# Cross-attention and linear attention on one core: one visit of values and ones per unit, and one running sum of the exponentials

## The reference, cut to what matters

```python
def layer0(q, k, v):                       # q = x, k = v = ctx
    Q, K, V = (heads(a @ W.T + b) for ...) # 4 x 16 x 1024 x 32
    score = einsum('bhqd,bhkd->bhqk', Q, K) / sqrt(32)
    att = softmax(score, axis=-1)
    out = einsum('bhqk,bhkd->bhqd', att, V) @ Wo.T + bo
    return layernorm(out + q) * gamma0 + beta0

def layer1(query, key, value):             # query = layer 0's result, key = value = ctx
    Q_phi, K_phi = elu(query), elu(key)
    KV = einsum('bnd,bne->bde', K_phi, value)
    Z = 1.0 / (einsum('bnd,bd->bn', Q_phi, K_phi.sum(axis=1)) + 1e-6)
    return layernorm(query + einsum('bnd,bde->bne', Q_phi, KV) * Z[..., None]) * gamma1 + beta1
```

## Time and profile before

| | |
|---|---|
| median of 3 runs | 1592.95 us |
| the profiled execution | 1593.17 us, span 1591.9 us |
| TensorE (PE) busy | 1542.1 us, 97% |
| VectorE (DVE) busy | 1225.6 us, 77% |
| GpSimd (POOL) busy | 1098.2 us, 69% |
| ScalarE (ACT) busy | 821.5 us, 52% |
| value matmuls L469 / ones matmuls L476, busy | 256.2 / 80.5 us |
| mean granted TensorE clock | 0.985 |

### The profile page before, as it was taken

One profiled execution on the slowest core, in us unless ns is written; L12 is line 12 of the kernel. 1 busy time (PEld: TensorE's weight loads), 2 busy tenths in 40 slices (PEclk: granted clock), 3 DMA queues, 4 the chain that ended last, 5 costly groups with the idle time before them and its releaser, 6 DMA issues.

```text
span 1591.9 us, 30289 instructions
## 1 busy us (share of the span) xinstructions
PE 1542.1 (97%) x10912; PEld 1037.1 (65%) x10912; DVE 1225.6 (77%) x2399; ACT 821.5 (52%) x1577; POOL 1098.2 (69%) x1012
## 2 busy tenths in 40 slices
PE   7989999999999999999999999999999999999996
PEld 5756667676766767667676676667667666766552
DVE  3767776767788787976778788886777877798887
ACT  1454554544555555655455455655455555565541
POOL 0365765657778787866678787776678878786881
PEclk9999999999999999999999999999999999999999
DMA  8634235351523426244242524425242342410000
GB/s 241 204 127 141 87 91 162 111 144 42 156 77 104 122 80 187 69 124 130 78 117 64 160 83 125 148 72 155 70 133 74 102 132 89 135 61 28 14 29 33
DMA packets 160340, 171.06 MB, mean 107 GB/s; under 512 B 21824, under 2 KB 122176, under 8 KB 160192
## 3 DMA queue, kind: packets, MB, share of 16 engines
q1 hardware_dynamic: 155968, 167.30, 34.9%
q10 hardware_dynamic: 4224, 1.84, 0.5%
HBM read 126.10 MB, written 42.99 MB: 106 GB/s over the span
## 4 chain that ended last, share of the span: by engine, by line
PE 89%; DVE 4%; DMA 2%; issue 2%; POOL 1%; ACT 1%; SPq 0%; ACTq 0%; DVEq 0%; POOLq 0%
PE score L437 15%; PE acc L469 15%; PE scoreT L451 14%; PE misc L510 7%; PE misc L522 7%; PE misc L486 7%; PE misc L538 7%; PE misc L499 7%; PE misc L546 6%; PE acc L476 3%; DVE maxes L739 1%; PE misc L530 1%; DMA bv_col<-bv_in 1%; ACT p_ring L612 1%; DMA ctx_nat<-ctx_in 0%
## 5 line engine op out<-in xcount | busy, mean ns | idle before, releaser
L969 POOL TENSOR_TENSOR pair_sum<-p_ring 128x512 f32<-128x512 f32 x512 | 664.4, 1308 | 366.4 <-DVE pair_sum L772 209.6
L612 ACT ACTIVATE p_ring<-scoreT 128x512 f32<-128x512 f32 x1024 | 602.1, 596 | 609.1 <-PE scoreT L451 603.8
L739 DVE TENSOR_REDUCE maxes<-score 128x1 f32<-128x512 f32 x1024 | 682.6, 679 | 236.8 <-PE score L437 232.2
L437 PE MATMUL score<-k_stack,q_stack 96*128 96x512 f32 x1024 | 647.0, 632 | 21.8 <-DVE maxes L739 15.6
L451 PEld LDWEIGHTS scoreT<-q_stack,k_stack 104*128 104x128 f32 x2048 | 386.5, 192 | 186.4 <-ACT p_ring L612 106.6
L451 PE MATMUL scoreT<-q_stack,k_stack 104*128 104x256 f32 x2048 | 427.1, 290 | 6.1 <-ACT p_ring L612 5.5
L437 PEld LDWEIGHTS score<-k_stack,q_stack 96*128 96x128 f32 x1024 | 194.1, 190 | 197.3 <-issue 141.6
L469 PE MATMUL acc<-p_ring,v_sb 128*32 128x256 f32 x4096 | 256.2, 392 | 0.0
L469 PEld LDWEIGHTS acc<-p_ring,v_sb 128*32 128x32 f32 x4096 | 122.3, 112 | 89.0 <-issue 9.4
L976 POOL TENSOR_TENSOR pair_sum<-pair_sum 128x512 f32<-128x512 f32 x128 | 163.9, 1281 | 0.0
L510 PE MATMUL misc<-wv,ctxT_sb 128*128 128x128 f32 x1024 | 134.8, 275 | 0.2 <-DVE k_low L812 0.2
(11 more groups left out here) (81 smaller groups left out, 1232.2 us busy)
## 6 DMA issues: line engine op xcount, KB each, us to landing
xT_sb<-xT_in SPq DMA_DIRECT2D x62, 512.0 KB, 3.7
k_stack<-k_dram SPq DMA_DIRECT2D x96, 256.0 KB, 4.2
q_stack<-q_dram SPq DMA_DIRECT2D x192, 128.0 KB, 2.5
k_dram<-k_high SPq DMA_DIRECT2D x32, 256.0 KB, 2.2
k_dram<-k_low SPq DMA_DIRECT2D x32, 256.0 KB, 2.2
q_dram<-q_high SPq DMA_DIRECT2D x64, 128.0 KB, 1.7
q_dram<-q_low SPq DMA_DIRECT2D x64, 128.0 KB, 1.9
ctx_nat<-ctx_in SPq DMA_DIRECT2D x32, 256.0 KB, 4.9
```

What stands on the lines that cost most here:

```text
L437: pe.matmul(score[k % 3][:], q_stack[0:SPLIT, unit % NQ, j, t * P:(t + 1) * P], k_stack[0:SPLIT, group_of[unit] % 2 * QUAD + j, h * HALF:( ...
L612: act.activation(p_ring[:, n % NP, h * HALF:(h + 1) * HALF], scoreT[k % 2][:], ACT.Exp, scale=SCALE).then_inc(A["exped"], 1)
L739: dve.reduce_max(maxes[:, unit % 2, t, j, h:h + 1], score[k % 3][:], AX.X).then_inc(V["maxed"], 1)
L969: pool.tensor_tensor(pair_sum[:, place_of_pair(pair), cols], p_ring[:, (n - 1) % NP, cols], p_ring[:, n % NP, cols], ALU.add).then_inc(L[" ...
```

## The change

One visit per unit in place of two, at `LEAD + 16`, after all eight steps: thirty-two value matmuls, then four ones matmuls over one sum of all eight steps, `exp_sum`. That sum is run up in place, step by step: GpSimd adds the low half of each of steps 1 to 7 and the high half of steps 4, 5 and 6; VectorE adds the high half of steps 1, 2, 3 and 7. `p_ring` grows from 8 places to 9, and an exponential into a place waits for the unit's ones. In the tick of a visit and the one after it the planner books up to 50 units of cost, and in the tick after it the finishing steps stand ahead of that tick's exponential and maximum. Keys' and queries' low halves are kept a tick later, with the DMAs that store them. The choice between the two ends of a layer norm is open to all tiles. Some distances of the planner change with it.

```diff
-    NQ, NP, NO, NX = 3, 8, 19, 3
+    NQ, NP, NO, NX = 3, 9, 19, 3
-    VISIT_AT = LEAD + 13
+    VISIT_AT = LEAD + UT
+    HIGH_ON_POOL = (4, 5, 6)
+    HIGH_ON_DVE = (1, 2, 3, 7)
-        TILE_TICKS = 21
+        TILE_TICKS = 20
...
+        def span(k):
+            return 50 if visiting(k) is not None else 14
         def find(name, engine, k, cost):
-            steps = when.setdefault(name, {})
-            while k in steps or room[engine].get(k, 0) + cost > (26 if visiting(k) is not None else 14):
+            steps, load = when.setdefault(name, {}), room[engine]
+            while k in steps or load.get(k, 0) + cost > span(k) and (
+                    load.get(k, 0) > span(k) - 4 or
+                    load.get(k, 0) + cost + load.get(k + 1, 0) > span(k) + span(k + 1)):
                 k += 1
...
-            if tile >= TILES - KT and ended_on_dve < find(f"shift{norm}", "POOL", scaled + 2, 13):
+            if ended_on_dve < find(f"shift{norm}", "POOL", scaled + 2, 13):
...
-                put = send("put_queries", end + 1, i, 2, False)
+                put = send("put_queries", end + 2, i, 2, False)
...
-            def visit(v):
+            def visit(unit):
...
+                pe.wait_ge(A["v_kept"], 2 * (group + 1))
+                if unit > 0:
+                    pe.wait_ge(V["out_scaled"], unit)
+                for kt in range(KT):
+                    n = KT * unit + kt
                     pe.wait_ge(A["exped"], 2 * (n + 1))
...
-                pe.wait_ge(L["quad_low"], v + 1)
-                pe.wait_ge(V["quad_high"], v + 1)
+                pe.wait_ge(L["low_added"], (KT - 1) * (unit + 1))
+                pe.wait_ge(V["high_on_dve"], len(HIGH_ON_DVE) * (unit + 1))
...
                 if h == 0 and n >= NP:
-                    act.wait_ge(T["weighted"], (n - NP) // VISIT + 1)
-                    act.wait_ge(L["paired"], 2 * ((n - NP) // 2 + 1))
+                    act.wait_ge(T["divided"], (n - NP) // KT + 1)
...
+            def add_high(unit, kt):                      # VectorE
+                n, cols = KT * unit + kt, slice(HALF, 2 * HALF)
+                before = exp_sum[:, cols] if kt > 1 else p_ring[:, (n - 1) % NP, cols]
+                if kt - 1 in HIGH_ON_POOL:
+                    dve.wait_ge(L["high_on_pool"], len(HIGH_ON_POOL) * (unit + 1))
+                elif kt > 1:
+                    dve.wait_ge(V["high_on_dve"], len(HIGH_ON_DVE) * unit + HIGH_ON_DVE.index(kt))
+                elif unit > 0:
+                    dve.wait_ge(T["divided"], unit)
+                dve.wait_ge(A["exped"], 2 * n + 2)
+                dve.tensor_tensor(exp_sum[:, cols], before, p_ring[:, n % NP, cols],
+                                  ALU.add).then_inc(V["high_on_dve"], 1)
...
+            def add_low(unit, kt):                       # GpSimd; its add_high is the same on the high columns
+                n, cols = KT * unit + kt, slice(0, HALF)
+                before = exp_sum[:, cols] if kt > 1 else p_ring[:, (n - 1) % NP, cols]
+                if kt > 1:
+                    pool.wait_ge(L["low_added"], (KT - 1) * unit + kt - 1)
+                elif unit > 0:
+                    pool.wait_ge(T["divided"], unit)
+                pool.wait_ge(A["exped"], 2 * n + 1)
+                pool.tensor_tensor(exp_sum[:, cols], before, p_ring[:, n % NP, cols],
+                                   ALU.add).then_inc(L["low_added"], 1)
...
             for k in range(FIRST, LAST):                 # ScalarE, and VectorE alike
+                if visiting(k - 1) is not None:
+                    finishing(k)
                 if 0 <= k - LEAD < HALVES:
                     exponential(k - LEAD)
...
+                if visiting(k - 1) is None:
+                    finishing(k)
```

More of the change, by code:

```diff
@@ L207, in book @@
             when[name][k] = tile
-            take(engine, k, cost)
+            rest = max(0, room[engine].get(k, 0) + cost - span(k))
+            take(engine, k, cost - rest)
+            take(engine, k + 1, rest)
             return k
@@ L309, in follow @@
             take("ACT", end, cost[0])
[L310 removed]
+            take("DVE", end + (kind in "KQ"), cost[1])
             if kind == "Q" and i > 0:
[L312 removed]
+                put = send("put_queries", end + 2, i, 2, False)
                 if i < NQ:
```

183 lines of the change are left out of this document (85 added, 98 removed).

## The result

The changed kernel takes 1670.84 us (median of 4 runs, 1661.55 to 1672.6), the kernel before 1592.76 us on the same chip: a ratio of 1.048, 95% interval 1.044 to 1.052. It is slower by 78 us where 16 us less was forecast, and it lies outside the range.

What follows compares the result with a forecast made beforehand. TensorE was taken as the bound, and VectorE where TensorE isn't. The terms -46.7 + 10 + 24 - 6 + 3 = -15.7 us gave 1577 us against the median of 1592.95, range 1550 to 1612.

Steps and rivals of the forecast that it cites:

- Does VectorE fit? +10 us: VectorE's added work against stages of four units: nearly fits at 98% busy; the fullest stages and units cost +10 us.
- The step before it: Price of VectorE's sum adds: 1.1 us each, 256 of them, +176 us of VectorE time (+68 to +347).
- Visits, -46.7: TensorE's visits go from 128 to 64; each of 64 units saves 0.73 us of ones and changeover, -46.7 us.
- The ones' wait: Ones matmuls waiting for GpSimd's last adds: seven adds take 9.2 us, 10.6 us are available, so 0.
- My own mark for being wrong: Stated sign of a wrong forecast: the ones wait above 10 us in all.
- VectorE's time, 1426: VectorE's total busy time after the change: 1225.6 + 176 for adds + 24 for finishing = 1426 us.
- Bare ticks, +24: Ticks with neither piece nor visit rise from 166 to 225; 59 more at 0.41 us of waiting, +24 us (0 to 36).
- Finishing, +24 us of VectorE: 12 more of 64 normalisations end on VectorE: 24 instructions of about 1 us, +24 us of VectorE time.
- The end, -6: After the last visit: attend 28 and phi 28 now stand ahead of it, visits finish five ticks earlier, -6 us (0 to -12).
- Clock, +3: TensorE's granted clock falls to half twice more, behind longer runs of bare ticks, +3 us (0 to 34).
- VectorE becomes the bound, slower: Rival: bare ticks, new and old, cost more as VectorE's adds fill it; +27 us, 1620 us, chance 0.22.
- TensorE stays the bound: Rival: VectorE's new work fits into its waits and bare ticks cost nothing more; 1540 us, chance 0.15.

Runs made afterwards that it cites:

- e12: The kernel before, with only each visit's first pair added and the other sum adds left out: 1601.1 us, ratio 1.004.
- e6: The change with all adds left out but VectorE's first high and GpSimd's first low one of each unit: 1533.3 us, ratio 0.962.
- e1: The change with finishing as before, only the last batch's layer norms may end on VectorE: 1664.8 us, ratio 1.045.
- e8: The change with the score matmul of each bare tick issued twice into the same bank: 1668.6 us, ratio 1.047.
- e3: The change with VectorE's four adds a unit left out, GpSimd's ten kept: 1575.7 us, ratio 0.989.
- e5: The change with VectorE's adds replaced by bn_stats on the same columns, one SBUF input, not held by GpSimd: 1597.5 us, ratio 1.001.

## Why the prediction was wrong

- **"Does VectorE fit? +10 us"** is the step that failed. I compared VectorE's work in four units with their length and trusted one unit that ran at 98%. The 10 us were charged to three of sixteen stages and to three full units. The ticks with pieces grew by 78.5 us, 22 of them for phi, while VectorE was busy for 83% and waited 225 us for scores. An average over four units hides that VectorE keeps up for some four ticks behind a visit and is 2.4 to 3.3 us late in the eight before the next: with three banks of scores TensorE then waits, and VectorE's idle time behind a visit does not pay for the late part. The step before it had the size (1.1 us an add; 1.00 measured), but I charged it only to full units.
- **Visits, -46.7.** Right as a mechanism, too small without the sums: there the merged visit, order and end are worth 1533.3 - 1601.1 = -68 us against e12, its partner, and -60 against the kernel before, whose sums hold VectorE (-52.7 with the end's 6 forecast). With the sums, what is over a bare tick fell by 35.0, since some 15 us of it are the ones' wait. Ones took 39.8 us (40.3).
- **The ones' wait, "it fits; I take 0".** Wrong by 11 to 15 us: 20 of 64 sets of ones wait 11.1 us in the rows above, and by the starts of values and ones it is 15.3 us. I put GpSimd's chain at 1.31 us an add; its low adds behind the first take 1.41, and VectorE's last add 1.59 in the stretch shown. My own mark for being wrong, over 10 us, was met.
- **VectorE's time, 1426.** Measured 1385.8: the adds +151 for +176.
- **Bare ticks, +24.** +29.6 measured, close. But I took only these for the place where VectorE bounds.
- **Phi.** Not in my sum: the transposes wait 29.4 us for it, 21.5 more; their 27 ticks take 1.87 us for 1.04.
- **Finishing, +24 us of VectorE.** It costs about 6 us of time (e1). **The end, -6**: -2.4 from the last score on, -5.1 from the last ones. **Clock, +3**: the mean fell to 0.959, beyond my two more stretches, but as a consequence (e8).
- **The rivals.** "VectorE becomes the bound, slower" had the sign and the adds' hold as its reason, and its 1620 us was 51 short for the same cause: it charged the bare ticks and left the ticks with pieces at the same 10 us. My case against it, the unit at 98%, was the poor witness. "TensorE stays the bound", 1540, is what e6 shows (1533) without sums.

## What to carry to other kernels

Before a sum is moved to another engine, look at where in the cycle that engine is late, not at its busy share over several cycles: with a few buffers between two engines, idle time on one side of the cycle does not pay for work on the other. Price a VectorE operation on two SBUF tiles by what GpSimd does at that moment, and charge its hold also to what is queued behind it. An experiment that leaves the moved work out (e3) and one that does it unheld (e5) tell in two runs what its length and its hold cost; ticks sorted by their distance from a visit tell where. Count what a planner moves with each edit before comparing two versions.
